# A GNN and mixture-of-experts layer on one core: the early rows' search is moved ahead of a chunk's marks, TensorE sums the marks' sub-tiles, and the probabilities take three operations

## The reference, cut to what matters

```
# x: 4096 x 128, adj: 4096 x 4096 with many zeros
filt   = tanh(adj * adj) * (adj > 0)
keep the 350 largest of each row of filt (most rows have fewer than 350 non-zeros)
h2     = tanh(layernorm(x) @ W_proj + b_proj)
x      = x + relu(new_adj @ (h2 @ W_gcn) + b_gcn)

s      = layernorm(x) @ Wg.T + bg                 # 8 experts
top 2 of 8, softmax over the two
x      = x + sum over the two experts of p_e * (relu(xn @ W1[e].T + b1[e]) @ W2[e].T + b2[e])
```

## Time and profile before

| | us |
|---|---|
| median of 3 runs | 470.61 (468.95 to 470.99) |
| the profiled execution | 468.27 |
| its span, first to last instruction | 466.5 |
| TensorE busy | 396.0 |
| VectorE busy | 366.1 |
| ScalarE busy | 339.5 |
| POOL busy | 205.6 |

### The profile page before, as it was taken

How to read it: one execution, slowest core, us unless ns; L and a number is a source line. 1 busy time by engine, 2 the same in 40 slices (tenths; PEclk the granted TensorE clock), 3 DMA queues, 4 the chain that set the end, 5 groups by cost and what they waited for, 6 DMA issues and landing times.

```text
span 466.5 us, 8103 instructions
## 1 busy us (share of the span) xinstructions
PE 396.0 (85%) x2456; PEld 242.2 (52%) x2456; DVE 366.1 (78%) x959; ACT 339.5 (73%) x345; POOL 205.6 (44%) x266
## 2 busy tenths in 40 slices
PE   0999989999788789999998979969798989999600
PEld 0455534444334244455454434436698989989500
DVE  5999978998999999985999999999976444444235
ACT  2789998889979778859999769973565656666400
POOL 3049961000004501800740638821777777777700
PEclk9999999999999979999999999989999999999955
DMA  7839976778357666873875757854745655631069
GB/s 227 328 120 373 351 290 231 265 279 306 136 193 257 227 225 228 274 260 145 302 253 211 259 191 279 288 137 75 109 91 161 106 114 107 92 79 51 23 218 326
DMA packets 57074, 95.42 MB, mean 205 GB/s; under 512 B 36740, under 2 KB 44088, under 8 KB 48832
## 3 DMA queue, kind: packets, MB, share of 16 engines
q1 hardware_dynamic: 45840, 79.80, 52.7%
q0 software_dynamic: 6048, 12.72, 9.0%
q10 hardware_dynamic: 5136, 2.30, 1.7%
HBM read 77.90 MB, written 12.67 MB: 194 GB/s over the span
## 4 chain that ended last, share of the span: by engine, by line
DVE 50%; PE 23%; issue 12%; DMA 5%; ACT 4%; POOL 4%; ACTq 1%; SPq 1%; DVEq 0%; POOLq 0%
DVE marks L856 17%; PE bank L1350 5%; ACT tbuf L1091 3%; PE bank L1438 3%; PE bank L1458 3%; PE bank L1459 3%; PE bank L1460 2%; PE bank L1440 2%; PE bank L1439 2%; POOL expert_rows L631 2%; DMA tbuf<-expert_rows 2%; DVE rowbf L707 2%; PE bank L1297 2%; DVE tbuf L1012 2%; DVE nrm L780 1%
## 5 line engine op out<-in xcount | busy, mean ns | idle before, releaser
L1350 PE MATMUL bank<-tbuf,g_sb 128*128 128x512 f32 x512 | 236.0, 609 | 2.5 <-ACT tbuf L1095 1.6
L617 POOL DMA_INDIRECT routed_rows<-aug,slots x64 | 87.9, 1373 | 153.3 <-DVE base L834 135.6
L1350 PEld LDWEIGHTS bank<-tbuf,g_sb 128*128 128x128 f32 x512 | 95.6, 195 | 111.8 <-issue 104.7
L856 DVE SCALAR_TENSOR_TENSOR marks<-abuf,marks 128x2048 bf16<-128x2048 int32 x56 | 129.4, 2312 | 1.1
L1091 ACT ACTIVATE tbuf<-abuf 128x2048 f32<-128x2048 f32 x64 | 121.5, 1898 | 4.8 <-PE bank L1350 2.6
L1095 ACT ACTIVATE tbuf<-tbuf 128x2048 f32<-128x2048 f32 x64 | 122.3, 1911 | 2.0
L631 POOL DMA_INDIRECT expert_rows<-abuf,xmeta x78 | 76.8, 985 | 23.8 <-issue 22.0
L1012 DVE SCALAR_TENSOR_TENSOR tbuf<-bank,tbuf 128x512 f16<-128x512 f32 x78 | 50.2, 685 | 45.8 <-ACT tbuf L1198 43.0
L1458 PE MATMUL bank<-w2h,tbuf 128*128 x312 | 54.4, 219 | 2.4 <-DVE tbuf L1012 2.4
L1460 PE MATMUL bank<-w2h,tbuf 128*128 x312 | 54.3, 219 | 0.0
L1459 PE MATMUL bank<-w2l,tbuf 128*128 x312 | 54.3, 219 | 0.0
(11 more groups left out here) (216 smaller groups left out, 434.3 us busy)
## 6 DMA issues: line engine op xcount, KB each, us to landing
abuf<-in_adj_tiles SPq DMA_DIRECT2D x64, 1024.0 KB, 5.5
wstage<-in_w POOLq DMA_DIRECT2D x16, 256.0 KB, 6.5
tbuf<-expert_rows SPq DMA_DIRECT2D x8, 512.0 KB, 7.3
out<-xres ACTq DMA_DIRECT2D x8, 256.0 KB, 6.3
expert_rows<-abuf,xmeta POOLq DMA_INDIRECT x78, 2.3
routed_rows<-pad SPq DMA_DIRECT2D x9, 130.0 KB
routed_rows<-aug,slots POOLq DMA_INDIRECT x64
abuf<-routed_rows SPq DMA_TRANSPOSE x39
```

The costliest lines, as they stand in the source:

```text
L617: pool.indirect_dma_start(xs, bass.IndirectOffsetOnAxis(ap=slots[:, i % 2, k * SUB + cc:k * SUB + cc + 1], axis=0), aug[:, i % 2, k, cc, : ...
L856: dve.scalar_tensor_tensor(mark, bits_in, 1.0, mark, ALU.min, ALU.add).then_inc(s_raw, 1)
L1350: last = pe.matmul(ps_feat[ib % 2][:, :], g_sb[:, c, :], tbuf[:, buf, cc, :], start=(c == 0), stop=(c == C - 1))
```

## The change

It has five parts.

1. VectorE's search step is moved from behind the chunk's marks to the head of the chunk, ahead of the routing's ready steps and the marks.
2. The three compare-and-accumulate instructions of a step become one compare of all three candidates (128 x 384) and one reduce, with a wait between them.
3. TensorE's sum of a step's counts is moved from the head of the next chunk to the middle of the same chunk, between its second and third sub-tile.
4. The two adds that fold the marks are gone; TensorE takes 16 instead of 4 matmuls of one column per block, and waits for the marks alone.
5. In the probabilities, the scale is put into the first operation, the reciprocal writes where it is used, and the two copies of `dest` into the rows move from VectorE to POOL, at the head of each scatter.

```diff
 def scatter(i, rs):                                  # POOL
+    pool.wait_ge(rs.cut, 2 * i + 2)
+    for k in range(2):
+        last = pool.tensor_copy(aug[:, q, k, :, D].bitcast(i32), dest[:, k, b * SUB:(b + 1) * SUB])
+    last.then_inc(rs.to, 1)
+    pool.wait_ge(rs.to, i + 1)
 def count_candidates(f, r, b):                       # VectorE
-    for k in range(1, 4):
-        last = dve.tensor_scalar(rowbf[:, k, :], rowval[:, :], cand[:, k:k + 1].bitcast(fp32), None,
-                                 ALU.is_ge, ALU.add, accum_out=ncand[:, k:k + 1])
-    last.then_inc(f.part, 1)
+    rlink(f, r, dve.tensor_tensor(
+        rowbf[:, 1:4, :], rowval[:, :].rearrange("p (o s) -> p o s", o=1).to_broadcast([P, 3, P]),
+        cand[:, 1:4].bitcast(fp32).rearrange("p (k o) -> p k o", o=1).to_broadcast([P, 3, P]), ALU.is_ge))
+    dve.tensor_reduce(ncand[:, 1:4], rowbf[:, 1:4, :], AX.X, ALU.add).then_inc(f.part, 1)
 def probabilities(i, rs):
-    for k in range(2):
-        dve.tensor_copy(aug[:, q, k, :, D].bitcast(i32), dest[:, k, b * SUB:(b + 1) * SUB])
-    link(dve.tensor_scalar(p1[:, :], ex[:, :], 1.0, None, ALU.add))
-    link(dve.reciprocal(p1[:, :], p1[:, :]))
-    link(dve.tensor_scalar(p1[:, :], p1[:, :], 1.0 / (WS * WX), None, ALU.mult))
-    dve.tensor_copy(aug[:, q, 0, :, D + 1], p1[:, :])
-    dve.tensor_tensor(aug[:, q, 1, :, D + 1], ex[:, :], p1[:, :], ALU.mult).then_inc(rs.meta, 1)
+    link(dve.tensor_scalar(p1[:, :], ex[:, :], 1.0, WS * WX, ALU.add, ALU.mult))
+    link(dve.reciprocal(aug[:, q, 0, :, D + 1], p1[:, :]))
+    dve.tensor_tensor(aug[:, q, 1, :, D + 1], ex[:, :], aug[:, q, 0, :, D + 1], ALU.mult).then_inc(rs.meta, 1)
 def mark_positive(n):
-    if k == NK - 1:
-        dve.wait_ge(s_raw, n + 1)
-        dve.tensor_tensor(mark[:, 0:2, :], mark[:, 0:2, :], mark[:, 2:4, :], ALU.add).then_inc(s_ind, 1)
-        dve.wait_ge(s_ind, 2 * ib + 1)
-        dve.tensor_tensor(mark[:, 0, :], mark[:, 0, :], mark[:, 1, :], ALU.add).then_inc(s_ind, 1)
 def ready_steps(n):                                  # now ahead of the marks
+    if STEP0 < n <= TIE:
+        raise_threshold(early, 0, n - STEP0 - 1)
+    if STEP0 <= n < TIE:
+        count_candidates(early, 0, n - STEP0)
+    if n == TIE:
+        count_ties(early, 0)
 def chunk_features(n):                               # TensorE
     for cc in range(CK):
+        if STEP0 <= n < TIE and cc == CK // 2:
+            total_candidates(early, 0, n - STEP0)
 def block_counts(ib):
-    pe.wait_ge(s_ind, 2 * ib + 2)
+    pe.wait_ge(s_raw, (ib + 1) * NK)
     for s in range(SUB):
-        last = pe.matmul(counts_of(ib)[:, s:s + 1], marks[:, ib % 2, 0, s * P:(s + 1) * P],
-                         ones_bf[:, 0:1], start=True, stop=True)
+        for cc in range(CK):
+            last = pe.matmul(counts_of(ib)[:, s:s + 1], marks[:, ib % 2, cc, s * P:(s + 1) * P],
+                             ones_bf[:, 0:1], start=(cc == 0), stop=(cc == CK - 1))
```

More of the change, by code:

```diff
@@ L275, in gnn_moe_layer @@
         s_raw = sem("s_raw")
-        s_ind = sem("s_ind")
         s_pe = sem("s_pe")
@@ L317, in __init__ @@
                 self.ns = sem("s_ns" + v)
+                self.to = sem("s_to" + v)
                 self.xn = sem("s_xn" + v)
@@ L611, in scatter @@
             def scatter(i, rs):
+                q, b = i % 2, ORDER[i]
+                pool.wait_ge(rs.cut, 2 * i + 2)
[3 more added lines that the diff above has]
+                pool.wait_ge(rs.to, i + 1)
                 pool.wait_ge(rs.sl, i + 1)
@@ L617, in scatter @@
                         pool.indirect_dma_start(
-                            xs, bass.IndirectOffsetOnAxis(ap=slots[:, i % 2, k * SUB + cc:k * SUB + cc + 1], axis=0),
-                            aug[:, i % 2, k, cc, :], None).then_inc(rs.scat[i % 2], 16)
+                            xs, bass.IndirectOffsetOnAxis(ap=slots[:, q, k * SUB + cc:k * SUB + cc + 1], axis=0),
+                            aug[:, q, k, cc, :], None).then_inc(rs.scat[q], 16)
             unit_column()
@@ L675, in _ @@
                     normal_group(g)
-            CHAIN = 2 + 3 * STEPS + 1 + 4 + R
+            CHAIN = 2 + 4 * STEPS + 1 + 4 + R
             TOTS = STEPS + 1
@@ L811, in choose_second, with probabilities @@
                 dve.tensor_tensor(ex[:, :], m2[:, :], m1[:, :], ALU.subtract).then_inc(rs.df, 1)
-            def probabilities(i, b, rs):
+            def probabilities(i, rs):
                 q = i % 2
-                for k in range(2):
-                    dve.tensor_copy(aug[:, q, k, :, D].bitcast(i32), dest[:, k, b * SUB:(b + 1) * SUB])
                 dve.wait_ge(rs.ex, i + 1)
-                link(dve.tensor_scalar(p1[:, :], ex[:, :], 1.0, None, ALU.add))
-                link(dve.reciprocal(p1[:, :], p1[:, :]))
-                link(dve.tensor_scalar(p1[:, :], p1[:, :], 1.0 / (WS * WX), None, ALU.mult))
-                dve.tensor_copy(aug[:, q, 0, :, D + 1], p1[:, :])
-                dve.tensor_tensor(aug[:, q, 1, :, D + 1], ex[:, :], p1[:, :], ALU.mult).then_inc(rs.meta, 1)
+                link(dve.tensor_scalar(p1[:, :], ex[:, :], 1.0, WS * WX, ALU.add, ALU.mult))
+                link(dve.reciprocal(aug[:, q, 0, :, D + 1], p1[:, :]))
+                dve.tensor_tensor(aug[:, q, 1, :, D + 1], ex[:, :], aug[:, q, 0, :, D + 1], ALU.mult).then_inc(rs.meta, 1)
             def assign(i, rs):
@@ L963, in route_steps @@
                     if n == START[i] + AT_PROB:
-                        probabilities(i, b, routed)
+                        probabilities(i, routed)
                     if n == START[i] + AT_ASSIGN:
@@ L989, in _ @@
                     square_rows(early, 0)
-                if STEP0 < n <= TIE:
-                    raise_threshold(early, 0, n - STEP0 - 1)
-                if STEP0 <= n < TIE:
-                    count_candidates(early, 0, n - STEP0)
-                if n == TIE:
-                    count_ties(early, 0)
                 if n == TIE + 1:
@@ L1061, in _ @@
                     choose_second(i, b, rerouted)
-                    probabilities(i, b, rerouted)
+                    probabilities(i, rerouted)
                     assign(i, rerouted)
@@ L1389, in _ @@
                     block_counts(n // NK - 1)
-                if STEP0 < n <= TIE:
-                    total_candidates(early, 0, n - 1 - STEP0)
                 if n == TIE + 1:
```

## The result

| us | before | after |
|---|---|---|
| median of 7 runs each | 469.00 | 465.26 |
| lowest and highest | 468.75, 470.99 | 464.59, 467.58 |
| the profiled execution | 468.27 | 466.88 |
| its span | 466.5 | 465.1 |
| the mask starts | 188.55 | 189.75 |

The changed kernel takes 0.9919 of the time before, with a 95% interval of 0.9897 to 0.9942: 3.7 us less. The interval lies wholly beyond the 0.5% that the prediction took for no change, the time lies in the range that it stated, and the gain that it forecast, 2.7 us, is the interval's lower end. The two profiled executions differ by 1.4 us only: before's took less than any of its 7 timed runs, and after's was the third highest of its own. All runs, here and in the experiments, read as fast ones.

What follows compares the result with a forecast made beforehand. VectorE was taken to bound 107 to 189 and 218 to 323.8 us, then POOL. +2.2 us at the mask, -5.3 behind it and +0.4 for POOL's copies gave -2.7: 470.61 to 467.9 us, range 463.8 to 472.6.

Steps and rivals of the forecast that it cites:

- second part: Stream from 107 to 189 us, up to the early rows' mask: VectorE sets the pace; +2.2 us at the mask.
- first part: Stream up to 107 us: an earlier weight split ends a TensorE wait, less the added counts; -0.4 us.
- search, operations: Search steps on VectorE: compare and reduce cost 1.07 instead of 0.80 us, over 15 steps +4.0 us.
- search, place: Search start: first count waits 3.1 instead of 1.01 us, the 0.60 us wait goes; together +1.5 us.
- The fourth part: Stream from 218 to 323.8 us: VectorE sets the pace; adds -3.2 and probabilities -2.1 us, together -5.3.
- no named wait of VectorE from 218 to 323: Expected sign in the profile after: VectorE runs without named waits up to the assignment that releases POOL.
- seven times they lie in POOL's waits: POOL's added copies, 0.4 us a pair: hidden seven times; the eighth, between the stores, costs +0.4 us.
- the tiles' end move by no less than POOL's start: Sign of being wrong: the end of the experts' tiles moving by less than POOL's start.
- A: Rival, 218 to 323.8 us: half of the 5.3 us lost to ScalarE, TensorE or loads; 470.6 us; chance 0.22.
- B: Rival, search: cheap reduce and compare, or shrinking TensorE waits; +1.4 instead of +4.0, 465.3 us; chance 0.16.
- C: Rival, search: TensorE's half-rate clock after waits makes VectorE wait for sums; +6.2 us, 474.1 us; chance 0.08.
- D: Rival, search: compare with two broadcast operands costs the upper end, +8.7 instead of +4.0, 472.6 us; chance 0.12.

Runs made afterwards that it cites:

- e4: Changed kernel with the three old compare-and-accumulate instructions in the search's new place; ratio 0.9840 to the kernel before, -7.8 us.
- e6: Changed kernel with search step behind the marks and TensorE's sum at the next chunk's head, new operations kept; ratio 0.9895 to the kernel before, -4.9 us.
- e3: Kernel before with only the search changes: new place, one compare and one reduce, TensorE's sum in mid-chunk; ratio 1.0089, +4.5 us.
- e8: Kernel before with the marks' adds removed and the probabilities changed, search wholly as before; ratio 0.9833, -9.4 us.
- e1: Kernel before with only the marks' adds removed, 16 TensorE matmuls a block instead; ratio 0.9880, -6.7 us.
- e2: Kernel before with only the probabilities changed: three operations, copies of dest on POOL; ratio 0.9967, -2.0 us.
- e0: Changed kernel run again without edit, with a further profile; ratio 0.9933 to the kernel before, -3.8 us.
- e5: Changed kernel with ScalarE's tanh of the early rows ahead of chunk 18's square; ratio 0.9882 to the kernel before, -5.7 us.
- e9: Kernel before with adds removed, probabilities changed and ScalarE's tanh of the early rows ahead of chunk 18's square; ratio 0.9851, -8.0 us.
- e7: Changed kernel with both the old compare-and-accumulate instructions and the earlier tanh of the early rows; ratio 0.9802 to the kernel before, -8.8 us.
- e10: Changed kernel run a third time without edit, with a further profile; ratio 0.9951 to the kernel before, -3.3 us.

## Why the prediction was right, and which terms were off

It was right in sign and in the main mechanism: VectorE set the pace in both parts, the search cost at the mask, and the adds and probabilities paid it back behind it. That POOL's end came within 0.3 us of the forecast is partly luck. The mask came 1.0 us less late than predicted and the stretch behind it gave 1.5 us less than predicted, and the two errors mostly cancel. By its own terms, in us, the second part counted from the head:

| term | predicted | measured | from |
|---|---|---|---|
| first part | -0.4 | -0.57 | head 99.62 to 99.05 |
| search, operations | +4.0 | +3.48 | after less e4 |
| search, place | +1.5 | +1.31 | after less e6 |
| the whole search | +5.5 | +4.96, +4.94 | e3 less before, after less e8 |
| adds, second part | -2.1 | -2.20 | e1 |
| probabilities, second part | -0.8 | -0.83 | e2 |
| at the mask | +2.2 | +1.20 | both profiles |
| mask to POOL | -5.3 | -3.83 (-4.88 in e0) | both profiles |
| of it, VectorE without a wait | -5.3 | -5.37 | e0, gate to places |
| of it, places later for TensorE | 0 | +1.03 (0 in e0) | after less e0 |
| of it, POOL's start behind VectorE | 0 | +0.49 | 0.77 less 0.28 |
| POOL's copies | +0.4 | +0.31 | its timeline |
| POOL's last end | -2.7 | -2.38 | both profiles |

**The search** was over-estimated by 0.5 us of 5.5, nearly all in the operations. Each of them was sized rightly (a step is 0.25 longer where +0.27 was taken). That 15 x 0.25 = 3.75 became 3.48 at the mask is e4's doing, which lost one step's gain in chunk 24; e6 less e8 has 3.63.
The choice of the fp32 reduce as the nearest row, and not of the bf16 add, was the step on which this rested. The reduce of 384 bf16 elements takes 556 ns, an add of 512 takes 425, and the fp32 reduce of 312 takes 466. The Trainium skill, "VectorE: DVE Perf Modes", perf-mode tier table, has the reduce at one element per cycle whatever the type. The row agrees: 556 ns lie by the fp32 reduce, whose 466 ns were scaled to 541, and not by the add.

**The place**: the wait of 3.1 us was 3.46, the 0.60 us behind it went. TensorE's waits of 4.1 and 5 us were 4.20 and 4.72. VectorE indeed never waited for the sums after that.

**The fourth part** is where steps failed. The work that VectorE saves was sized rightly. Counted from the gate to the places it is 110.39 us before and 105.02 in e0, 5.37 less; 0.35 of them are the wait in before's profile that e3 too hasn't got, so the adds and probabilities gave 5.0 of the 5.3.

The first failed step is "no named wait of VectorE from 218 to 323". In the changed kernel TensorE waits 3.10 us for the normalised rows of the seventh block, then takes 5.30 us for a chunk, with the clock at the lower level for most of it, and its last chunks follow without a gap up to the counts of places, which are ready at 319.58. VectorE arrives 0.9 us before them, and counted from the gate the places start 1.03 us later than in e0. The sum had no term for TensorE's own path to these counts. In the kernel before, the clock fell there too (0.50 at 308 to 310), but TensorE was ready 1.07 us ahead of VectorE. In after VectorE comes 4.15 us earlier, and TensorE only 2.18. Every profile that has the adds gone and shows the clock fall there has the wait (e1 0.30, e8 0.76, e5 0.82, e4 0.85, e9 0.93, after 0.94, e6, e7 and e10 0.95 us); e0, with the same wait of TensorE but full clock, has none, and neither has e3, with the fall and the adds. e2 has neither the fall nor a wait. A chunk of 3.60 instead of 5.30 us would have put after's counts 0.8 us ahead of VectorE, as in e0. Taking away the fall by itself wasn't tried.

The second is "seven times they lie in POOL's waits", said of POOL's copies. The copies themselves do, but part 5 makes POOL start 0.49 us later behind VectorE, in every profile that has it, and at the seventh block that stands in the path to the end. It is also 0.49 of the 0.54 us by which e2 stayed behind the predicted 2.1 there. Which of its instructions costs it, the copies or the waits added with them, isn't settled.

The three together give the measured number: -5.37 + 1.03 + 0.49 = -3.85, against -3.84 from the gate to POOL.

e1 and e2 alone gain 3.58 and 1.56, together 5.14, but in one kernel (e8) 4.18. About half of the difference is e8's longer wait (0.76 against e1's 0.30). The other half, 0.49, is there at the marks of chunk 63 already; 0.3 of it lies between the marks of chunks 58 and 59, where three of VectorE's small operations take 0.24, 0.35 and 0.23 us instead of 0.16. Why isn't settled.

One of the prediction's signs of being wrong goes against its own sum. It asked that the tiles' end move by no less than POOL's start, and its sum had 2.7 for the one and 3.1 for the other; they moved by 2.38 and 2.63.

**The rivals.** A (the fourth part gives half): its mechanism exists, with 0.94 us of TensorE instead of 2.6 us lost; ScalarE's wait for VectorE's cut fell from 2.72 us to 0.68, so ScalarE still had room, as argued against it. B (cheap operations) and D (a dear compare) fall with 558 and 556 ns. C (the clock) was right that the lower level would come after the new waits, and its price didn't come, for VectorE didn't feel it in the search: where it came VectorE had routing and marks to do, 3.00 of 3.00 us. Nor did a chunk behind such a wait take twice its 3.5 us: the one in chunk 61 took 5.30. That is where it cost something, and where the prediction hadn't looked.

**The time.** 467.9 us was said and 465.3 measured. Of these 2.6 us, 1.6 are the starting point: the 3 runs of before had a median of 470.61, all 7 have 469.00. The last 1.0 is the gain, 3.7 by the medians against 2.7. The profiles alone give 2.4 at POOL's last end; the two others of the changed kernel put POOL's start at 320.57 and 322.50, the three on average at 321.4, again 2.4 us ahead of before's single one. Before's profile took 0.7 us less than its median, so that 3.1 is what these marks say of the medians, inside the interval of 2.7 to 4.8. Where the other 0.6 of the 3.7 lies isn't shown.

## What to carry to other kernels

Moving a step ahead in an in-order queue gains only up to its second latest input, and everything behind it waits with it: read both inputs before moving it, and try the move apart from the change of operations. One wide operation isn't by itself a saving over three narrow ones: three compares with an accumulator of 128 took 0.80 us, one compare and one reduce of 384 took 1.06. A change that gives back elsewhere what it costs here should be split by parts: this one was faster by 3.7 us and hid a part of +4.5.

## What the runs showed of the hardware

- After the same wait of 3.10 us of TensorE, ended by the same instruction, the granted clock was 0.51 at 308 to 310 us in one profile of the changed kernel and 1.00 in another. In e2, after 3.48 us, it was 1.00 there; after 4.20 us it was 0.50 from 124 to 127. A wait of 3.1 to 3.5 us by itself doesn't decide it here.
- Small copies on POOL took 0.18 to 0.24 us, but in three of the changed kernel's eight pairs the first took 2.15 to 2.18. Each of these starts within 0.2 us after a mark of 2.28 us has started on VectorE (the copy at 203.79 beside the following row of VectorE's timeline):

```profile
203.64 4.68 DVE L858 SCALAR_TENSOR_TENSOR marks<-abuf,marks 128x2048 bf16<-128x2048 int32 x2
```

  The copy ends 0.05 us after the first of the two marks. The marks themselves didn't get longer (2311 ns, 2312 before), so it was POOL that waited. The Trainium skill, "SBUF — State Buffer", section "SBUF: two separate sides", describes this: of a VectorE operation with two SBUF inputs and a GpSimd operation, the first to start holds the shared ports for its whole length. The trace agrees, with 2.18 us. All three lay in POOL's waits and cost nothing; the prediction had weighed only the other direction, VectorE held by POOL.
- The pause between VectorE's last operation of an assignment and POOL's first indirect DMA, which waits for it, was 0.28 us in the kernels without part 5 and 0.77 in those with it, at five blocks of each profile.
- 16 matmuls of one column take 0.55 us where 4 took 0.25: 0.025 us for each further one.
